# Full attention on one core: maxima negated and turned outputs copied by ScalarE, outputs divided by GpSimd, VectorE left with the maxima

## What is computed

```
q = (x @ Wq.T + bq).reshape(b, s, 16, 8)      # likewise k, v; s = 1024
w = jnp.einsum('bshd,bzhd->bhsz', q, k) / jnp.sqrt(8.)
w = jax.nn.softmax(w, axis=-1)                # exp(w - max) / sum
vw = jnp.einsum('bhsz,bzhd->bshd', w, v)
out = vw.reshape(b, s, 128) @ Wo.T + bo
```

## Time and profile before

| | |
|---|---|
| time, median of three runs | 2060.09 us (2059.11 to 2060.32) |
| profiled execution: first to last instruction (span) | 2056.4 us |
| its own time | the span and what lies around it: the median is 3.7 us above the span |
| busy over the span | PE 77%, DVE 65%, ACT 55%, POOL 27% |
| the stage's first reduce to its last division | 958.2 to 1637.7 us |
| its 256 steps, first product to last | 990.3 to 1634.7 us |
| granted clock, mean over the span | 0.870 |

### The profile page before, as it was taken

One profiled execution on the slowest core, in us unless ns is written; L12 is line 12 of the kernel. 1 busy time (PEld: TensorE's weight loads), 2 busy tenths in 40 slices (PEclk: granted clock), 3 DMA queues, 4 the chain that ended last, 5 costly groups with the idle time before them and its releaser, 6 DMA issues. The chain is left out here.

```text
span 2056.4 us, 34421 instructions
## 1 busy us (share of the span) xinstructions
PE 1579.5 (77%) x11512; PEld 917.7 (45%) x11512; DVE 1339.0 (65%) x3318; ACT 1135.7 (55%) x2965; POOL 550.2 (27%) x615
## 2 busy tenths in 40 slices
PE   6799999999991699245999999999999735424910
PEld 3478777777771699221222222222222234323910
DVE  5655656656564322267999999999999287842523
ACT  3366766666651344142688888888888733111300
POOL 2133323524526400571001001001000020372056
PEclk9799999999995799666899999999999967556965
DMA  5144311211101676142000000000000000013832
GB/s 191 39 156 156 107 30 36 54 28 43 42 21 37 203 234 205 52 122 83 23 21 26 18 26 18 27 18 26 19 25 2 1 0 6 21 45 124 253 91 72
DMA packets 86203, 138.99 MB, mean 68 GB/s; under 512 B 18084, under 2 KB 57252, under 8 KB 85900
## 3 DMA queue, kind: packets, MB, share of 16 engines
q1 hardware_dynamic: 62860, 92.08, 15.2%
q0 software_dynamic: 11936, 34.49, 5.1%
q10 hardware_dynamic: 11232, 10.23, 1.4%
HBM read 75.51 MB, written 45.11 MB: 59 GB/s over the span
## 5 line engine op out<-in xcount | busy, mean ns | idle before, releaser
L2062 DVE TENSOR_REDUCE q_max<-s_ps 128x1 f32<-128x1024 f32 x512 | 598.2, 1219 | 14.0 <-PE s_ps L1953 6.8
L2043 ACT ACTIVATE probs<-s_ps 128x512 f32<-128x512 f32 x1024 | 535.5, 603 | 124.5 <-PE s_ps L1974 124.3
L1953 PE MATMUL s_ps<-k_stack,q_stack 64*128 64x512 bf16 x1024 | 351.2, 397 | 16.9 <-PEq L96 8.5
L1974 PE MATMUL s_ps<-q_stack,k_stack 64*128 64x512 bf16 x1024 | 319.5, 384 | 20.2 <-ACT probs L2043 15.8
L1988 PE MATMUL o_ps<-probs,v_aug 128*32 128x512 f32 x2048 | 273.6, 606 | 0.7 <-ACT probs L2043 0.7
L1974 PEld LDWEIGHTS s_ps<-q_stack,k_stack 64*128 64x128 bf16 x1024 | 78.6, 94 | 333.9 <-ACT probs L2043 281.9
L989 POOL TENSOR_TENSOR probs<-probs,p_rsum 128x512 f32<-128x512 f32 x128 | 132.9, 1038 | 325.8 <-DVE p_rsum L966 325.1
L869 ACT ACTIVATE probs<-s_biased,s_min 128x128 f32<-128x128 f32 (+1 forms) x512 | 197.7, 391 | 37.0 <-DVE s_min L960 35.6
L734 PE MATMUL score_ps<-k_pad,q_bd 128*128 128x128 f32 x1024 | 146.7, 287 | 0.0
L960 DVE CUSTOM_DVE_ANT_0 s_biased<-score_ps,nbias 128x128 f32<-128x128 f32 (+1 forms) x512 | 115.8, 282 | 41.8 <-PE score_ps L734 40.6
L1580 POOL CAST neg_max_parts<-neg_max 16x128 bf16<-16x128 f32 x32 | 9.0, 281 | 474.7 <-DVE neg_max L2070 474.7
(11 more groups left out here) (315 smaller groups left out, 2824.5 us busy)
## 6 DMA issues: line engine op xcount, KB each, us to landing
moe0b_wblock<-in_L_ffn_blocks SPq DMA_DIRECT2D x39, 578.0 KB, 3.9
moe_rows<-zero_rows POOLq DMA_DIRECT2D x18, 960.0 KB, 4.4
moe1b_wblock<-in_L_ffn_blocks SPq DMA_DIRECT2D x39, 256.0 KB, 3.5
v_shift<-v_tiles SPq DMA_DIRECT2D x32, 256.0 KB, 3.1
v_shift<-v_tiles SPq DMA_DIRECT2D x32, 224.0 KB, 3.6
qk_parts_dram<-qk_parts SPq DMA_DIRECT2D x16, 384.0 KB, 2.7
q_stack<-qk_parts_dram SPq DMA_DIRECT2D x192, 32.0 KB
k_stack<-qk_parts_dram SPq DMA_DIRECT2D x192, 32.0 KB
```

Of the source, the lines that this page charges most:

```text
L1953: mm = nc.tensor.matmul(s1[u % 2][:, c * CH:(c + 1) * CH], qs[head_rows(m), quad % 4, j, qt * P:(qt + 1) * P], ks[head_rows(m), quad % 4, ...
L1974: nc.tensor.matmul(bank_of("exp", 4 * k + pos)[:], ks[head_rows(m), quad % 4, j, kt * P:(kt + 1) * P], qs[head_rows(m), quad % 4, j, half ...
L2043: nc.scalar.activation(pr[:, k % 2, HEADS[pos], :], bank_of("exp", n)[:], ACT.Exp).then_inc(sm["exp"], 1)
L2062: v.tensor_reduce(mx[:, h % 4, col:col + 1], s1[u % 2][:], AX.X, ALU.max).then_inc(sm["maxed"], 1)
```

## The change

DVE keeps only the 512 reductions. ACT negates the turned maxima (an ACTIVATE Copy with scale -1) and copies the whole turned bank to a new SBUF buffer o_unscaled of two slots; POOL then does the division from this copy, as a power of -1 and a multiplication. The bank of the turned output is free (o_done) after ACT's copy, that of the turned maxima (m_neg) after ACT's negation; the new semaphore divided frees the slots of the copy. On ACT both stand behind the first exponential (position 0) of the step after the turn. PE's order, the rotation of the banks and SP's queue stay as they were.

```
+        od = K.sb("o_unscaled", [P, 2, CH], ctx=st)
+        negone = K.sb("neg_one", [P, CPT, 4], ctx=st)
@@ gpsimd
+                def divide(m):
+                    ...
+                    pool.wait_ge(sm["o_done"], m + 1)
+                    heads = od[:, m % 2, :].rearrange("p (t h c) -> p t h c", h=4, c=32)
+                    ...
+                    nc.gpsimd.tensor_tensor(ro[:, m % 2], heads[:, :, :, HD1], negone[:], ALU.pow).then_inc(sm["o_rsum"], 1)
+                    pool.wait_ge(sm["o_rsum"], m + 1)
+                    nc.gpsimd.tensor_tensor(
+                        K.nat[...], heads[:, :, :, 0:HD1], bc(ro[:, m % 2], 3, HD1), ALU.mult).then_inc(sm["divided"], 1)
...
+                    if quad >= 2:
+                        divide(2 * quad - 3)
                     if quad >= 1:
                         split_max(2 * quad - 1)
+                        divide(2 * quad - 2)
                     split_max(2 * quad)
+                divide(2 * NQ - 3)
                 split_max(2 * NQ - 1)
+                divide(2 * NQ - 2)
+                divide(2 * NQ - 1)
@@ scalar
+                def negate_max(h):
+                    act.wait_ge(sm["m_turned"], h + 1)
+                    if h >= 1:
+                        act.wait_ge(sm["m_split"], 4 * h)
+                    nc.scalar.activation(nm[:], turned_view(bank_of("m_neg", h))[0:HU, 0, :], ACT.Copy, scale=-1.0
+                                         ).then_inc(sm["m_neg"], 1)
+                def output_turned(m):
+                    act.wait_ge(sm["o_turned"], m + 1)
+                    if m >= 2:
+                        act.wait_ge(sm["divided"], m - 1)
+                    nc.scalar.copy(od[:, m % 2, :], bank_of("o_done", m)[:]).then_inc(sm["o_done"], 1)
+                negate_max(0)
                 for k in range(NK):
                     for pos in range(4):
                         ...
                         nc.scalar.activation(pr[:, k % 2, HEADS[pos], :], bank_of("exp", n)[:], ACT.Exp
                                              ).then_inc(sm["exp"], 1)
+                        if pos == 0 and k >= 1 and max_done_at(k - 1) is not None:
+                            negate_max(max_done_at(k - 1))
+                        if pos == 0 and k >= 1 and output_due_at(k - 1) is not None:
+                            output_turned(output_due_at(k - 1))
                         if pos == 2 and k % TPB == 0 and k >= TPB:
                             output(k // TPB - 1)
...
                 output(2 * NQ - 1)
+                output_turned(2 * NQ - 1)
@@ vector
-                def negate_max(h): ...
-                def divide(m): ...
                 for u in range(AHEAD):
                     reduce_max(u)
-                    if u == HU:
-                        negate_max(0)
                 for k in range(NK):
                     for u in step_units(k):
                         reduce_max(u)
-                    if max_done_at(k) is not None:
-                        negate_max(max_done_at(k))
-                    if output_due_at(k) is not None:
-                        divide(output_due_at(k))
-                divide(2 * NQ - 1)
```

More of the change, by code:

```diff
@@ L1765 @@
             "m_stored", "m_loaded",
-            "s2_mm", "exp", "v_aug", "pv_mm", "o_out", "o_turned", "o_done", "o_rsum")
+            "s2_mm", "exp", "v_aug", "pv_mm", "o_out", "o_turned", "o_done", "negone_set", "o_rsum", "divided")
 def full_attention_stage(nc, K, A, wo, M):
@@ L1925, in split_max @@
                            nr[:])
+                def divide(m):
+                    quad, half = divmod(m, 2)
+                    b, s = divmod(quad, QUADS)
+                    pool.wait_ge(sm["o_done"], m + 1)
+                    heads = od[:, m % 2, :].rearrange("p (t h c) -> p t h c", h=4, c=32)
+                    t = b * TPB + half * CPT
+                    if m >= 2:
+                        pool.wait_ge(sm["divided"], m - 1)
+                    nc.gpsimd.tensor_tensor(ro[:, m % 2], heads[:, :, :, HD1], negone[:], ALU.pow).then_inc(sm["o_rsum"], 1)
+                    pool.wait_ge(sm["o_rsum"], m + 1)
+                    nc.gpsimd.tensor_tensor(
+                        K.nat[:, t:t + CPT, s * 32:(s + 1) * 32].rearrange("p t (h d) -> p t h d", d=HD1),
+                        heads[:, :, :, 0:HD1], bc(ro[:, m % 2], 3, HD1), ALU.mult).then_inc(sm["divided"], 1)
                 wo.gate(pool)
+                nc.gpsimd.memset(negone[:], -1.0).then_inc(sm["negone_set"], 1)
+                pool.wait_ge(sm["negone_set"], 1)
                 for quad in range(NQ):
@@ L2044, in _ @@
                                              ).then_inc(sm["exp"], 1)
+                        if pos == 0 and k >= 1 and max_done_at(k - 1) is not None:
+                            negate_max(max_done_at(k - 1))
+                        if pos == 0 and k >= 1 and output_due_at(k - 1) is not None:
+                            output_turned(output_due_at(k - 1))
                         if pos == 2 and k % TPB == 0 and k >= TPB:
                             output(k // TPB - 1)
+                if max_done_at(NK - 1) is not None:
+                    negate_max(max_done_at(NK - 1))
                 output(2 * NQ - 1)
+                output_turned(2 * NQ - 1)
             @block.vector
```

## The result

The changed kernel takes 2099.59 us (median of 4 runs, 2097.3 to 2100.52) against 2059.6 before: a ratio of 1.0193, 95% interval 1.0178 to 1.0207. It is slower by 40 us. The forecast was 2100.4, or +40.3.

What follows compares the result with a forecast made beforehand. It took PE, ACT and the three shared banks to set the pace, with DVE following. Terms 25.1 + 14.3 - 2.4 - 0.3 + 3.6 = +40.3 us gave span 2096.7, plus 3.7 for the median: 2100.4, range 2096 to 2114.

Steps and rivals of the forecast that it cites:

- The loop of a plain step: Step without output or maximum work: claimed to close over PE and ACT alone, no reduction in it, staying at 2.39 us.
- the 1.41 us of DVE there: DVE's busy time in 30 us behind step 244, read as a negation and two divisions; steps there were no shorter.
- Copy of the turned output: Output steps: ACT's copy frees the bank 0.81 us later, step 2.97 to 3.78, 31 times: +25.1 us.
- Negation: Maximum steps: ACT's negation ends later, scores(k+1,2) start 0.46 us later, 31 times: +14.3 us (12.6 to 24).
- Off DVE: Steps behind output steps lose 0.08 us, 30 times: -2.4; stage start without DVE's first negation: -0.3 us.
- The three terms of the steps: Within the steps: copy +25.1, negation +14.3, and -2.4 us for the steps behind output steps.
- Division by POOL: Division of 3.6 us, power 3.0: hidden 31 times in the loop; the last, in the open, +3.6 us (2.2 to 3.9).
- the 7.8: Microseconds from the end of ACT's copy to the next split in POOL's queue, claimed to hide the division.
- the estimate of 1.1 us for the last division: Last division by the skill's ratio of about two, instead of 3.6 us; the sum would be 2.5 us lower.
- the rule on short waits for PSUM: Skill's account of a kernel whose clock went up and down from brief PSUM waits; by it, the clock rival would be forecast.
- The clock's fall: Rival, chance 0.03: PE's longer waits drop its clock to 1.2 GHz in the 62 longer steps, 81 us more, 2182.
- nothing waits for them: Plain steps: no wait for DVE's reductions claimed, so freeing them from queuing behind a division is worth nothing there.

## Why the prediction was right

*The loop of a plain step.* Right: 2.39 in the changed kernel, with reductions of half the length, and with either half of the change. One plain step of each half, that in which ACT also copies op (k = 8, 16, ..., 248), is 2.59 before and after alike; the working counts it with the others, which changes no term. Nor does a slip in reading: the 1.41 us of DVE there are the end of the last reduction (some 0.6), the negation and one division; the second lies behind the window.

*Copy of the turned output*, +25.1. The step was forecast as 3.78 and is 3.78 in 30 of 31 cases; the copy is 0.58 long and begins where the sum put it. Moving the copy by one exponential took the whole term away, and a copy shorter by 0.29 shortened the step by 0.29.

*Negation*, +14.3. Forecast 3.07, measured 3.07. The length read off the line between 64 and 512 columns, 0.27, is 0.25 in fact.

*Off DVE*, -2.4 and -0.3. The steps behind an output step are 2.39; the start gave 0.5, and the table load behind the first negation cost nothing that shows. The three terms of the steps make 37.0, and the steps grew by 36.8.

*Division by POOL*, nothing in the loop and +3.6 at the end. The power takes 2.9 instead of 3.0, the tail grew by 3.5, and doubling the power changed no step. The cover runs out between a division of 6.4 and one of 12.4 us; that is what the 7.8 and the 1.8 behind it would have, but no run lies closer to them. The factor of about two that the Trainium skill (GPSIMD Engine Reference, section 4.1, Engine selection) gives against GpSimd for adding, multiplying and maxima with two inputs made the estimate of 1.1 us for the last division; it took 3.3. The multiplication alone took 0.41 on POOL against 0.29 on DVE, less than that factor; the power, which the section doesn't name, took 2.90 against 0.26 for DVE's reciprocal.

*The clock.* From 992 us to the last product it was 1.00, with waits of 0.95 us on PE in the output steps; the rule on short waits for PSUM (the Trainium skill, TensorE: Matmul & The Clock Gate, section "A second HAM failure mode") did not come true here. The clock's fall, one of the rivals, was seen in another kernel all the same: with the power done four times and PE waiting 2.8 to 4.4 us at once (the rows are in the last section).

*The time around the span.* I added 3.7 us to the span for the median. Of that only 1.8 is time outside the span (the profiled run of after took 2097.3 with a span of 2095.5); the rest is that the profile of before was taken of a run some 1.9 us below its median, an estimate from the same 1.8. That of after lay 2.3 below its own, and that the two are alike is luck. So is part of the agreement to 0.8 us in all: the forecast span, 2096.7, was 1.2 too long, about what the earlier stages happened to be shorter. The steps, 37.0 against 36.8, owe nothing to either.

*What it left out.* That DVE does not set the length of a plain step does not mean that it has room: the experiments with the shorter copy showed that 0.3 us taken off one step of eight makes DVE the bound of the next. And "nothing waits for them", said of the reductions, is too strong. In the list of which the earlier trace rows is a line (total, times, longest) PE's first-pass matmuls do wait for DVE:

```profile
PEld s_ps L1953 <- DVE q_max L2062: 76.3, 178, 0.6
```

These waits end before that of scores(k+1,2) for the exponential, which is why halving the reductions took nothing off a plain step. By 2.36 of 2.39 us, DVE was 0.03 from setting the pace itself.

## What to carry to other kernels

A nearly full engine need not set the pace, even one that is full to 0.03 us in 2.39: look for a stretch of the same loop in which it has nothing to do, and compare the step lengths. When a shared buffer's reader moves to another engine, what counts is when the buffer is read out, which is the place in the new engine's queue and not the load; here one exponential earlier or later is worth 39 us. And when the bound of a step is relieved, ask how much room the next engine has before counting the gain.

## What was not expected of the hardware

After the last division the next stage begins with eight transposes. PE had then been idle for 5.74 us, before only for 1.86. The eight in after and in before, and a stretch of after as in the earlier trace rows:

```profile
1677.99 1.94 PE L2166 MATMUL wo_tps<-ident,nat 128*128 128x128 f32 x8 [5.74 <-PEq L96]
...
1638.93 1.06 PE L2146 MATMUL wo_tps<-ident,nat 128*128 128x128 f32 x8 [1.86 <-PEq L96]
...
1674.00:1684.00 10.00, 4.79 (x21) 4.42 (x22) 0.69 (x1) 1.07 (x2) 2.27 (x2) 0.50 0.02 1
```

In after the granted clock had fallen to 0.50, which is 1.2 GHz, while PE stood idle, so the eight took 0.9 us longer. Whether the whole time grew by this is not shown: the rest of the span behind the last division is 418.7 to 420.8 us in the kernels of this case, with the short tail as with the long one.

The clock fell within the loop too, where the power is done four times and PE waits for late maxima. One such wait, and a stretch behind it:

```profile
1249.14 0.39 PE L2004 MATMUL s_ps<-q_stack,k_stack 64*128 64x512 bf16 x1 [3.01 <-DMA q_stack<-neg_max_dram]
...
1250.40:1253.80 3.40, 3.40 (x20) 0.69 (x16) 2.92 (x4) 3.09 (x7) 0.00 (x0) 0.50 0.25 69
```

It happened in 14 of the 30 halves with such a wait, each time within 1.5 us of the wait's end, before or behind it, and the eight matmuls of a product then took up to 1.9 us instead of 1.06. Why it fell in these halves and not in the others is open.
